# Zeroing of the expert slots and sums in 28 pieces instead of 12, an expert's first-layer matrices loaded earlier, sums read back ring by ring

## The reference

```python
# scan over time, both directions, keys and values are fside; twice, with its own w and u
a = a * decay + exp(k) * v ; b = b * decay + exp(k)
out = sigmoid(r) * num / max(den, 1e-8) * (0.8 + 0.2 * tf)
# attention-like block: layer norm, three mixes with the token before, r/k/v products,
# output product, residual, second layer norm, second block (r2, relu(k2)^2, v2), residual
x = x + attn(cond(x, fside, fside, ...))
# expert layer on the second scan's result, 2048 tokens, 32 experts, 8 for each token
h = relu2(x_lat @ w1[e]) * weight          # x_lat = x @ fc1T, width 256
y_lat = sum over chosen experts of h @ w2[e]
x = x + relu2(x @ up) @ down + y_lat @ fc2T
```

## Time and profile before

| | us |
|---|---|
| median of 3 runs | 1288.86 |
| the profiled execution's own time | 1288.49 |
| its span, first to last instruction | 1286.4 |
| PE busy | 1106.0 (86%) |
| DVE busy | 734.9 (57%) |
| ACT busy | 460.8 (36%) |
| POOL busy | 595.3 (46%) |

### The profile page before, as it was taken

The page is one execution under the profiler, slowest core; times in us unless marked ns, Lnnn a source line. Parts: engine busy times, 40 slices in busy tenths (PEclk is TensorE's granted clock), DMA queues, the critical chain, the costliest instruction groups (busy, mean ns, idle before and its releaser), DMA issues.

```text
span 1286.4 us, 14175 instructions
## 1 busy us (share of the span) xinstructions
PE 1106.0 (86%) x3686; PEld 649.3 (50%) x3687; DVE 734.9 (57%) x1387; ACT 460.8 (36%) x694; POOL 595.3 (46%) x461
## 2 busy tenths in 40 slices
PE   0274499997998799889999989988999999999928
PEld 0131144433443344354544434437888888888813
DVE  8565458889998999870585000013444444444325
ACT  3352347444744474352221111102333343333401
POOL 3212304551455145620007666643777777777710
PEclk9977799998998899999999999998999999999959
DMA  3859921000301020301205645275777777777684
GB/s 132 295 181 359 359 75 50 18 24 4 119 16 24 1 90 17 133 1 53 79 9 176 231 161 197 102 244 115 130 126 128 128 122 132 122 129 128 80 249 164
DMA packets 125746, 157.57 MB, mean 122 GB/s; under 512 B 8720, under 2 KB 103952, under 8 KB 125712
## 3 DMA queue, kind: packets, MB, share of 16 engines
q1 hardware_dynamic: 96528, 117.83, 29.9%
q0 software_dynamic: 29184, 39.34, 16.4%
HBM read 79.67 MB, written 77.46 MB: 122 GB/s over the span
## 4 chain that ended last, share of the span: by engine, by line
PE 53%; DVE 19%; issue 8%; another core or an unknown queue 6%; DMA 5%; SPq 4%; ACT 2%; POOL 1%; DVEq 0%; POOLq 0%; ACTq 0%
PE banks L599 11%; PE banks L620 11%; PE banks L1595 8%; PE banks L528 8%; DMA arena<-fT 4%; PE banks L551 4%; DVE arena L1375 4%; DVE arena L1472 3%; PE banks L610 3%; PE banks L589 3%; PE banks L1613 2%; PE banks L511 2%; DVE arena L1356 2%; DVE arena L1383 1%
## 5 line engine op out<-in xcount | busy, mean ns | idle before, releaser
L1595 PE MATMUL banks<-arena 128*128 128x512 f32 x896 | 390.8, 597 | 28.3 <-ACT arena L1130 18.5
L473 POOL DMA_INDIRECT sums<-arena x160 | 249.6, 1560 | 121.4 <-ACT arena L726 90.6
L1595 PEld LDWEIGHTS banks<-arena 128*128 128x128 f32 x896 | 171.4, 192 | 245.6 <-issue 225.5
L461 POOL DMA_INDIRECT slots_in<-arena x128 | 129.2, 1009 | 102.5 <-issue 88.6
L599 PE MATMUL banks<-arena 128*128 x640 | 153.3, 383 | 8.7 <-issue 8.7
L528 PE MATMUL banks<-arena 128*128 128x512 f32 x320 | 146.8, 607 | 6.1 <-ACT arena L697 3.2
L620 PE MATMUL banks<-arena 128*128 x640 | 151.2, 379 | 0.0
L1613 PE MATMUL banks<-arena 128*128 128x512 f32 (+1 forms) x64 | 46.2, 888 | 96.4 <-DVE arena L1438 72.3
L881 DVE SCALAR_TENSOR_TENSOR arena<-arena 128x256 f32<-128x256 f32 x160 | 72.1, 490 | 98.1 <-ACT arena L711 98.1
L599 PEld LDWEIGHTS banks<-arena 128*128 128x128 f32 x640 | 116.5, 192 | 21.7 <-issue 8.9
L620 PEld LDWEIGHTS banks<-arena 128*128 128x128 f32 x640 | 115.4, 190 | 12.4
(11 more groups left out here) (179 smaller groups left out, 1366.0 us busy)
## 6 DMA issues: line engine op xcount, KB each, us to landing
slots_in<-arena SPq DMA_DIRECT2D x8, 2800.0 KB, 18.3
arena<-slots_in SPq DMA_DIRECT2D x80, 280.0 KB, 3.2
sums<-arena SPq DMA_DIRECT2D x4, 2176.0 KB, 20.4
arena<-fT SPq DMA_DIRECT2D x32, 256.0 KB, 2.7
arena<-xT SPq DMA_DIRECT2D x8, 1024.0 KB, 5.6
arena<-w2T SPq DMA_DIRECT2D x4, 2048.0 KB
arena<-sums SPq DMA_DIRECT2D x16, 512.0 KB, 8.4
arena<-w1T SPq DMA_DIRECT2D x2, 2048.0 KB
```

The lines of the kernel that those rows point to most:

```text
L461: pool.indirect_dma_start(rows_in, bass.IndirectOffsetOnAxis(ap=POSU[:, n, j:j + 1], axis=0), XLR[:, n], None).then_inc(S['scattered'], 16)
L473: pool.indirect_dma_start(sums[g % RING], bass.IndirectOffsetOnAxis(ap=DESTU[:, g:g + 1], axis=0), YO[:, i % 4, c], None, compute_op=ALU.add)\
L1595: ins = pe.matmul(out, w[:, k, m * P:(m + 1) * P], x[:, k], start=(k == 0), stop=(k == kt - 1))
```

## The change

Three things are done, with what they need in memory.

1. **Zeroing.** `slots_in` is zeroed in 20 pieces of 8 blocks (1120 KB) and the sum tables in 8 pieces of 8 or 9 tiles (1024 or 1152 KB). One piece follows each key load: 4 of slots in pass 0, 8 in pass 1, 8 in pass 2, and the 8 of sums in pass 3. `ZROW` has a place of its own, so `square(2, ...)` no longer waits. For that room EUV is one tile instead of two, and `bonus_num` waits until POOL has read the EUV of the item before (`num_ready`).
2. **Expert matrices.** The last two of DOWNW's 8 slices move to a tile of their own, DOWNT; their old place is free from the start of `down`, and w1T's experts 30 and 31 are asked for together with experts 0 to 7. The three loads of experts 24 to 29 stand ahead of the wait for `scattered`. PE does t1(0) and t1(1) ahead of the wait for DVE's last evacuation. DOWNT lies over ZROW's place, so `downT` is loaded behind the last zeroing.
3. **Sums.** The load of ring r for batch 0 is issued as soon as ring r's adds are done, and `combine` adds the buffers one by one. `latent(b+1)` stands between the third and the fourth product of `fc2(b)`.

```diff
-        EU, EUV = (place(2, T) for _ in range(2))
+        EU = place(2, T)
+        EUV = place(T)
...
-        ZROW = NR[:, 0, 0:ROW]
-        ZEROS = 8
+        ZROW = place(ROW)
+        ZEROS, ZEROED = 20, 2 * RING
...
+        DOWNT = place(2, C)
...
-            ld(sp, DOWNW, 'downT').then_inc(S['down_loaded'], 16)
+            sp.wait_ge(S['sums_zeroed'], 16 * ZEROED)
+            down = A['downT'].rearrange("(k p) d -> p k d", p=P)
+            sp.dma_start(DOWNW[:, 0:KS - 2], down[:, 0:KS - 2]).then_inc(S['down_loaded'], 16)
+            sp.dma_start(DOWNT, down[:, KS - 2:]).then_inc(S['down_loaded'], 16)
...
             load_w1(0, quarter)
+            load_w1(E - 2, 2)
             load_w2(1)
...
+            for k in range(0, KS - 2, 2):
+                sp.wait_ge(S['down_step'], (KS - 1) * (B - 1) + k + 2)
+                load_w1(E - KS + k, 2)
             sp.wait_ge(S['scattered'], 16 * NT * TOPK)
             for i in range(4):
                 xg_load(sp, i, i, 0)
-            for k in range(0, KS, 2):
-                if k + 2 < KS:
-                    sp.wait_ge(S['down_step'], (KS - 1) * (B - 1) + k + 2)
-                else:
-                    sp.wait_ge(S['down_mm'], K * B)
-                load_w1(E - KS + k, 2)
...
             for r in range(RING):
                 sp.wait_ge(y_added[r], 16 * (NB // RING))
-            for b in range(B):
+                if r == 0:
+                    sp.wait_ge(S['m1_mm'], NP)
+                load_sums(0, r)
+            for b in range(1, B):
                 for r in range(RING):
-                    sp.dma_start(YB[:, b, r], sums[r][b * T:(b + 1) * T].rearrange("(n p) d -> p n d", p=P))\
-                      .then_inc(sums_loaded[b], 16)
+                    load_sums(b, r)
...
-            pe.wait_ge(S['down_evac'], K * B)
             pe.wait_ge(S['up_relu'], KS * B)
             t1(0, 0, 0)
             t1(1, 1, 0)
-            pe.wait_ge(S['w1_loaded'], 16 * (4 + KS // 2))
+            pe.wait_ge(S['down_evac'], K * B)
+            pe.wait_ge(S['w1_loaded'], 16 * 8)
...
-            def fc2(b):
+            def fc2(b, between):
...
+                    if m == 2:
+                        between()
...
+            latent(0)
             for b in range(B):
-                latent(b)
-                fc2(b)
+                fc2(b, lambda: latent(b + 1) if b + 1 < B else None)
...
-                dve.wait_ge(sums_loaded[b], 16 * RING)
+                for r in range(2):
+                    dve.wait_ge(sums_loaded[b][r], 16)
                 step.did(dve.tensor_tensor(whole, YB[:, b, 0], YB[:, b, 1], ALU.add))
-                step.did(dve.tensor_tensor(YP[:, b % 2], YB[:, b, 2], YB[:, b, 3], ALU.add))
+                dve.wait_ge(sums_loaded[b][2], 16)
                 step.wait()
-                dve.tensor_tensor(whole, whole, YP[:, b % 2], ALU.add).then_inc(S['combined'], 1)
+                step.did(dve.tensor_tensor(whole, whole, YB[:, b, 2], ALU.add))
+                dve.wait_ge(sums_loaded[b][3], 16)
+                step.wait()
+                dve.tensor_tensor(whole, whole, YB[:, b, 3], ALU.add).then_inc(S['combined'], 1)
...
-                    if not prev:
-                        zero_slots(2 * n)
-                        zero_slots(2 * n + 1)
-                        zero_sums(n)
+                    if not prev and n == 0:
+                        sp.wait_ge(S['zero_ready'], 2)
+                    if nxt:
+                        zero_slots(8 * b + n - 4 if prev else n)
+                    else:
+                        zero_sums(n // 2, n % 2)
...
-                if which == 2:
-                    for q in range(2):
-                        act.wait_ge(S[f'slots_zeroed{q}'], 16 * ZEROS // 2)
-                    act.wait_ge(S['sums_zeroed'], 16 * RING)
...
-                dve.scalar_tensor_tensor(EUV[:, par], EU[:, par], dcol_of(caps, it), KV[:, par], ALU.min, ALU.mult)\
+                if not (isinstance(i, int) and i < 1):
+                    dve.wait_ge(S['num_ready'], i)
+                dve.scalar_tensor_tensor(EUV, EU[:, par], dcol_of(caps, it), KV[:, par], ALU.min, ALU.mult)\
```

More of the change, by code:

```diff
@@ L228, in build @@
         y_added = [sem(f"y_added{r}") for r in range(RING)]
-        sums_loaded = [sem(f"sums_loaded{b}") for b in range(B)]
+        sums_loaded = [[sem(f"sums_loaded{b}_{r}") for r in range(RING)] for b in range(B)]
         def item(i, half, b, k, w, par):
@@ L294, in build @@
         YR = place(NT, LAT)
-        YP = place(2, TT, LAT)
         assert top[0] <= end2
@@ L546, in down @@
                 if n == 0:
-                    pe.wait_ge(S['down_loaded'], 16)
+                    pe.wait_ge(S['down_loaded'], 32)
                 for m in range(K):
@@ L550, in down @@
                         pe.wait_ge(S['down_evac'], K * (b - 1) + m + 1)
-                    ins = pe.matmul(bank(DOWN_BANK[m]), DOWNW[:, k, m * P:(m + 1) * P], HS[:, k],
+                    ins = pe.matmul(bank(DOWN_BANK[m]), (DOWNW[:, k] if k < KS - 2 else DOWNT[:, k - KS + 2])[:, m * P:(m + 1) * P], HS[:, k],
                                     start=(k == 0), stop=(k == KS - 1))
@@ L982, in zero_slots, with zero_sums @@
                 per = SLOT_BLOCKS // ZEROS
-                if z == 0:
-                    sp.wait_ge(S['zero_ready'], 2)
-                sp.dma_start(slots_in[z * per:(z + 1) * per].rearrange("i p d -> p i d"),
+                sp.dma_start(slots_in[bass.ds(z * per, per)].rearrange("i p d -> p i d"),
                              ZROW.rearrange("p (o d) -> p o d", o=1).to_broadcast([P, per, ROW]))\
-                  .then_inc(S[f'slots_zeroed{z % 2}'], 16)
-            def zero_sums(r):
-                sp.dma_start(sums[r].rearrange("(i p) d -> p i d", p=P),
-                             ZROW[:, 0:LAT].rearrange("p (o d) -> p o d", o=1).to_broadcast([P, NT + 1, LAT]))\
+                  .then_inc(S['slots_zeroed'], 16)
+            def zero_sums(r, half):
+                tiles = (slice(0, NT // 2), slice(NT // 2, NT + 1))[half]
+                sp.dma_start(sums[r].rearrange("(i p) d -> p i d", p=P)[:, tiles],
+                             ZROW[:, 0:LAT].rearrange("p (o d) -> p o d", o=1).to_broadcast([P, tiles.stop - tiles.start, LAT]))\
                   .then_inc(S['sums_zeroed'], 16)
@@ L1043, in post @@
                 pool.wait_ge(S['euv_ready'], i + 1)
-                pool.tensor_tensor(F[:, par, 0], F[:, par, 0], EUV[:, par], ALU.add).then_inc(S['num_ready'], 1)
+                pool.tensor_tensor(F[:, par, 0], F[:, par, 0], EUV, ALU.add).then_inc(S['num_ready'], 1)
                 pool.wait_ge(S['inv_ready'], i + 1)
```

11 lines of the change are left out of this document (7 added, 4 removed).

## The result

The changed kernel takes 1252.48 us (median of 4 runs, 1250.67 to 1254.29); the kernel before took 1289.97 beside it (4 runs). The ratio is 0.9708, 95% interval 0.9685 to 0.9731. The profiled execution took 1251.29 us with a span of 1249.4, 37.0 less than before.

| stretch | before | after | difference | forecast |
|---|---|---|---|---|
| start to DVE's first scan of pass 0 | 83.2 | 80.9 | -2.3 | 0 |
| from there to the first scan of pass 1 | 110.5 | 89.5 | -21.0 | -21.5 |
| from there to the first `up` | 438.9 | 439.0 | +0.1 | +4.0 |
| first `up` to the end of the last `down` | 229.2 | 233.4 | +4.1 | 0 |
| from there to the first `m1`, and that `m1` | 14.8 | 4.7 | -10.1 | -9.8 |

A forecast was written before the change was run, and what follows sets the result against it. Mostly PE or the DVE-key-DVE loop of the scans has no gap, so only places where both stand still can pay: -21.5 + 4.0 - 9.8 - 8.8 = -36.1, from 1288.5 to 1252.4 us, range 1246 to 1264.

The forecast's parts named there:

- the price of part 1: Passes 1 to 3: keys with zeros behind them land 0.4 us later, paid in 10 items, +4.0 us.
- Part 1, the stalls, -21.5: Pass 0: DVE's waits of 13.46 and 8.57 us for keys behind zeros go, gaining 13.0 and 8.5 us.
- the second stall: Pass 0: DVE's wait of 8.57 us for a key, of which 8.5 us were taken as gained.
- The bound of 35 us: Passes 1 to 3: upper bound of the zeroing's cost if a whole piece delays the next key, 10 keys.
- Part 2, -9.8: First expert product: `m1` starts 7.9 us earlier and runs 1.9 us shorter at full clock; bounds 4 and 11.
- Part 3, -8.8: The end: transposes 7.6 us earlier, 2.2 us gained in later batches, less 1.0 us; bounds 3 and 11.
- the delay of the last add: The end: loads of sums running beside the adds make the last add 1.0 us later.
- My second rival: The end: adds and loads hold each other up, 5 us more than forecast, 1257.5 us; 10 in 100.
- Zeros that hamper the scans: Passes 1 to 3: each of 10 keys pays 2 us instead of 0.4, +16, 1268 us; 10 in 100.
- Something else in pass 0: Pass 0: gates on ACT, POOL or PE's last products leave half of 21.5 us gained, 1263 us; 7 in 100.
- Slower than before: Passes 1 to 3: keys served together with the piece behind land after 9.0 us, 1311 us; 3 in 100.

The follow-up runs named there:

- The part alone: The kernel before with only the 28 zeroing pieces, ZROW's own place and the single EUV, chip B: 1256.68 us, ratio 0.9843.
- Experiment 3: The kernel before with the new zeroing, but all 28 pieces left in pass 0: 1275.38 us, ratio 0.9996.
- Experiment 4: The changed kernel with the zero piece issued just before the key in passes 1 to 3: 1278.83 us, ratio 1.0017.
- A: First chip of all, where the kernel before took 1289.97 us and the changed kernel 1252.48 us, ratio 0.9708.
- B: Another chip (kernel before 1276.17 us); there the kernel before with only the expert-matrix change took 1267.79 us, ratio 0.9939.
- Experiments 7 and 8: Changed kernel without DOWNT, experts 30 and 31 loaded after `down`: ratio 0.9752; changed kernel with the third w1T load behind the first four slot loads: 0.9774.
- experiment 1: The changed kernel itself run again, unaltered, on another chip (D): 1250.04 us, ratio 0.9718 of the kernel before.

## Why the prediction was right, point by point

The time was forecast as 1252.4 and is 1252.5, but that close a hit is luck: the price of part 1 was 4 us too high, and `up` and `down` took 4 us more than the nothing I gave them, by waits that have nothing to do with the change.

- **Part 1, the stalls, -21.5.** Right. The traces show -21.0, the 13.46 became 0.65 where I left 0.5, and nothing took the place of the second stall. The part alone gave 20 us. Experiment 3 shows that it is the spreading.
- **Part 1, the price, +4.0.** The step that failed is that each key lands 0.4 us later and that this "is paid in full" in 10 items. Keys do land 0.2 later (2.9 against 2.7), but it costs nothing, 128.8 us a pass with and without. I read DVE's wait of 0.34 us in the earlier trace rows as a place without slack. It has some: the clip behind it took 1.13 us there and takes 0.43 elsewhere. POOL before, POOL and DVE after:

```profile
243.02 1.27 POOL L1048 TENSOR_TENSOR arena<-arena 128x512 f32<-128x512 f32 x1
```

```profile
219.75 1.27 POOL L1062 TENSOR_TENSOR arena<-arena 128x512 f32<-128x512 f32 x1
...
220.32 0.98 DVE L1366 TENSOR_SCALAR arena<-arena 128x512 f32<-128x512 f32 x1 [0.49 <-DMA arena<-fT]
221.22 1.27 DVE L1385 TENSOR_TENSOR_SCAN arena<-banks,arena 128x512 f32<-128x512 f32 x1
```

  POOL's operation ends at 244.29 and the clip at 244.58; after, at 221.02 and 221.30. The clip starts later against POOL and is shorter by as much: in both traces it ends 0.3 us behind POOL in each case where it begins well within POOL's operation; where it begins in that operation's last 0.1 us it takes its 0.43. By these rows, as an estimate, this key could land 0.7 us later for nothing (1.13 less 0.43). The Trainium skill, "SBUF — State Buffer", section "SBUF: two separate sides", says that DVE, in some of its operations, and GpSimd share a pair of ports as an exclusive lock, held for the whole instruction. The trace agrees: the clip that begins within POOL's operation ends behind it, and where the clip begins first, at 499.55 in the kernel before, POOL's operation of 499.56 is the longer one, 1.54 us instead of 1.27. That the duration holds the wait for the ports is my reading of these rows.
- **Part 1, where the other end lies.** The bound of 35 us was for a piece that delays the next key. Experiment 4 measures just that, 39.5: 14 keys without room, not 10.
- **Part 2, -9.8.** Right on A: -10.1, of which 1.8 is the clock, as forecast (1.9). On B it is 8, because the wait it removes is shorter there. Experiments 7 and 8 show that all eight loads must have landed by then; either of them late brings a wait for w1T of 3.8 to 4.8 us and the slow clock back. That the slots would be there as before held on A, but not in experiment 1, where their lateness alone cost the clock as well.
- **Part 3, -8.8.** Measured -7.7. The term that was mis-sized is the delay of the last add, "I take 1.0 us": it is 2.3 (5.98 against 3.68). The load of ring 3 took 4.52 where I took 4.4, and `latent` gave 2.5 for 2.2. My second rival, add and load holding each other up for 5 us more than forecast, is right in its first half: the add came 1.3 us later than forecast, and on A the load behind it was not held up. In other traces that load took up to 7.04 us, which these runs don't explain.
- **Not in the sum.** -2.3 at the start (clock) and +4.1 in `up` and `down`, both shown to come and go without the change. Without these two and without the price, the forecast was -40.1, against -38.7 measured (-21.0, +0.1, -10.1 and -7.7).
- **Rivals.** Zeros that hamper the scans: not at one piece, 5 us in a pass with three. Something else in pass 0: no. Slower than before: it takes the other order of key and piece, and then comes out 0.17% slower.

## What to carry to other kernels

A latency-critical load and bulk traffic can share a queue if the bulk always stands right *behind* the load, in portions that are through before the next one is asked for: one such piece cost nothing, in front it cost 2.8 us at each of the 14 keys without room. Before an operation is called free of slack, compare its duration there with the shortest of its kind: a part of that duration may be a wait that a later start only shortens. A wait of PE of several us (3.05, 3.8 and 4.8 here) is priced with the slow product behind it, and idle time of PE that can't be removed can be filled with products nobody reads (2.3 us here, by two traces). And when one wait is taken out, the one that was hidden behind it, here the last scatter's, becomes the next limit.

## What the runs showed of the hardware that was not expected

- A clip of 128x512 on DVE takes 0.43 us alone and up to 1.52 when it begins well within an operation of POOL of 1.27 us, ending 0.3 us behind it.
- An accumulating indirect DMA lands after 3.6 to 3.9 us alone (five kernels), and after 5.6 to 6.1 with 512 KB loads on SP's queue beside it (nine kernels).
- The same stage took 221.6 us on two chips and 226.5 to 233.4 on two others, in waits of PE of 0.9 to 4.2 us behind ACT and DVE, which began late without late work ahead of them, and in the slow clock that followed. The times of before on the four chips go the same way (1276 against 1287 to 1290), though this stretch holds 7.6 of the 13 us between A and B. Its cause is open.
